# A selective state-space scan with routed experts on one core: the front re-ordered, the work at the half boundaries re-ordered, and the state update moved ahead of the partition sum in the steps that scatter rows

## What is computed

```python
dt   = soft_clamp(softplus(xn @ Wdt.T + bdt), 0.001, 0.1, 0.5)
B, C = xn @ WB.T, xn @ WC.T
A    = -exp(soft_clamp(A_log, -5, 5, 0.5))
dA   = exp(soft_clamp(dt[..., None] * A, -8, 8, 0.5))
for t in range(1024):                        # the scan; h is (batch, channel, state)
    h = dA[t] * h + dt[t] * B[t] * x[t]
    h = h * min(20 / (norm(h) + 1e-8), 1)    # norm over all channels and states of a batch
    y[t] = h @ C[t] + Dp * x[t]
# experts: top 2 of 8 by xn @ w_g, at most 1280 rows each, softmax of the two logits
out = combine(gelu(rows @ c_fc[e]) @ c_proj[e])      # for every expert e
```

## Time and profile before

| stretch | us | what |
|---|---|---|
| 0 to 69.67 | 69.67 | front |
| 69.67 to 93.06 | 23.39 | steps 0 to 15 |
| 93.06 to 305.70 | 212.64 | steps 16 to 143, with 64 scatters |
| 305.70 to 1454 | 1148.30 | steps 144 to 927 |
| 1454 to 1620 | 166.00 | the rest of the steps, 64 of them with a fetch |
| 1620 to 1644.40 | 24.40 | tail |

### The profile page before, as it was taken

One profiled execution on the slowest core, in us unless ns is written; L12 is line 12 of the kernel. 1 busy time (PEld: TensorE's weight loads), 2 busy tenths in 40 slices (PEclk: granted clock), 3 DMA queues, 4 the chain that ended last, 5 costly groups with the idle time before them and its releaser, 6 DMA issues.

```text
span 1644.4 us, 34338 instructions
## 1 busy us (share of the span) xinstructions
PE 1282.0 (78%) x9628; PEld 1123.2 (68%) x9628; DVE 1532.7 (93%) x9635; ACT 1153.7 (70%) x2909; POOL 777.6 (47%) x1253
## 2 busy tenths in 40 slices
PE   5656445479989888989989998898989798855661
PEld 4445344368878777877978787797878688844550
DVE  7688888999999999999999999999999999987788
ACT  5877456486787768868776877778777777847450
POOL 5166776544444443444443344344444444468852
PEclk9776677789999999999989999999999999967895
DMA  9921111200111020111002002011100200012245
GB/s 319 315 83 50 42 44 43 98 15 30 43 49 43 16 75 22 36 62 37 30 16 87 23 25 73 24 37 41 57 22 24 66 30 17 17 39 73 73 149 194
DMA packets 85088, 104.56 MB, mean 64 GB/s; under 512 B 7712, under 2 KB 75936, under 8 KB 84896
## 3 DMA queue, kind: packets, MB, share of 16 engines
q1 hardware_dynamic: 76848, 85.47, 15.8%
q0 software_dynamic: 6144, 16.79, 3.2%
q10 hardware_dynamic: 1904, 0.09, 0.1%
HBM read 56.45 MB, written 45.88 MB: 62 GB/s over the span
## 4 chain that ended last, share of the span: by engine, by line
PE 48%; POOL 15%; ACT 14%; DVE 14%; issue 7%; DMA 2%; ACTq 0%; POOLq 0%; SPq 0%; DVEq 0%
PE ps L1219 15%; PE ps L1203 13%; PE ps L1191 8%; POOL arena L516 7%; PE ps L1185 5%; ACT arena L854 4%; POOL xg L496 4%; PE ps L1153 3%; DVE arena L724 2%; DVE arena L702 2%; DVE arena L718 2%; DVE arena L710 2%; DVE arena L696 2%; POOL wf L502 2%; PE ps L1069 2%
## 5 line engine op out<-in xcount | busy, mean ns | idle before, releaser
L516 POOL TENSOR_TENSOR arena<-arena,neghalf 128x1 f32<-128x1 f32 x1025 | 602.3, 588 | 798.4 <-DVE arena L699 751.1
L724 DVE SCALAR_TENSOR_TENSOR arena<-arena 128x128 f32<-128x128 f32 x1024 | 360.5, 352 | 23.5 <-POOL arena L516 23.5
L1191 PE MATMUL ps<-arena,pick 128*128 128x128 f32 x2048 | 301.9, 295 | 49.4 <-ACT arena L961 25.7
L1203 PE MATMUL ps<-arena,wf 128*128 128x256 f32 x1280 | 308.9, 393 | 20.3 <-ACT arena L974 9.4
L1191 PEld LDWEIGHTS ps<-arena,pick 128*128 128x128 f32 x2048 | 279.0, 210 | 62.8 <-ACT arena L961 50.1
L961 ACT ACTIVATE arena<-ps,arena 128x128 f32<-128x128 f32 x1024 | 292.3, 374 | 32.6 <-PE ps L1191 30.7
L710 DVE CUSTOM_DVE_ANT_0 arena<-arena 128x128 f32<-128x128 f32 x1024 | 293.3, 286 | 9.5 <-PE ps L1153 5.8
L702 DVE CUSTOM_DVE_ANT_0 arena<-arena 128x128 f32<-128x128 f32 x1024 | 299.1, 292 | 2.2
L1219 PE MATMUL ps<-wp,arena 128*128 128x256 f32 x1280 | 295.8, 385 | 3.1 <-ACT arena L974 3.1
L696 DVE TENSOR_TENSOR arena<-arena 128x128 f32<-128x128 f32 x1024 | 290.6, 284 | 0.0
L1203 PEld LDWEIGHTS ps<-arena,wf 128*128 128x128 f32 x1280 | 244.7, 198 | 53.5 <-ACT arena L974 10.2
(11 more groups left out here) (148 smaller groups left out, 1323.3 us busy)
## 6 DMA issues: line engine op xcount, KB each, us to landing
xg<-zeros SPq DMA_DIRECT2D x10, 1024.0 KB, 10.6
xrow<-xg SPq DMA_DIRECT2D x40, 256.0 KB, 2.7
yg<-arena SPq DMA_DIRECT2D x40, 256.0 KB, 2.1
arena<-in_x SPq DMA_DIRECT2D x16, 512.0 KB, 8.8
wf<-in_c_fc SPq DMA_DIRECT2D x8, 1024.0 KB, 5.1
wp<-in_c_proj SPq DMA_DIRECT2D x8, 1024.0 KB, 6.0
ys<-arena SPq DMA_DIRECT2D x66, 64.0 KB
xnd<-arena SPq DMA_DIRECT2D x8, 512.0 KB, 5.7
```

What stands on the lines that cost most here:

```text
L516: g.tensor_tensor(sv[:, slot, 1:2], mx, neghalf[:, 0:1], ALU.pow).then_inc(s_ready, 1)
L724: v.scalar_tensor_tensor(hr[:, slot, :], vv, sv[:, before, 1:2], ur[:, slot, :], ALU.mult, ALU.add)\
L1191: last = t.matmul(ps[2][:, j * P:(j + 1) * P], pick[:, q * QUAD + j, :], xin, start=True, stop=True)
L1203: last = t.matmul(ps[4 + j % 2][:, c * TS:(c + 1) * TS], wf[:, k, (2 * j + c) * P:(2 * j + c + 1) * P], xt[:, k, :], start=k == 0, stop=k ...
```

## The change

It has four groups of edits.

1. **Front.** The small loads are issued in another order (A_log and the two vectors first). GpSimd needs 12 constants instead of 17 before it turns to the powers; the select that builds `pick` is cut into four of 512 columns, placed behind the powers of chunks 2 to 5, and the others behind that of chunk 1. The state ring and the windows are no longer cleared by GpSimd but by ScalarE (`clear_states`, 128 by 2048 twice, and one copy for `win`). VectorE normalises chunk 0 before the statistics of chunk 1. TensorE makes the time rates of half 0 ahead of the second transposes. ScalarE's list is re-ordered, and of half 0 it takes only the Tanh of steps 0 to 15 ahead of the scan (`tanh_part`, 128 by 64); those of steps 16 to 63 (128 by 192) follow in quads 0 to 2. In the routing the softmax of the two logits moves behind the slots.
2. **First blocks.** The Tanh of half 1 go into quads 3 to 14 instead of 0 to 14; rates and logs of half 2 go from quads 1 and 2 to quads 5 and 6.
3. **Half boundaries.** `logs_of` is split: `rates_out`, which frees the PSUM bank, now comes ahead of two `decay_op`. The soft clamp moves from the end of a half's third block to its second quad. Input pieces start 3 steps later and avoid steps with a scatter or fetch while others are free.
4. **Steps with a scatter.** The update comes ahead of the partition sum; `following` of such a step moves into the next one, behind its product, and the next step's maximum behind its first reduction.

```diff
-                    if step in sending:
-                        dve.wait_ge(q_ready, now)
-                        v.tensor_scalar(mx, qv, 1.0, None, ALU.max).then_inc(m_ready, 1)
-                    dve.wait_ge(h_ready, now)
-                    v.tensor_tensor(vv, hr[:, before, :], da[:, slot, :], ALU.mult).then_inc(v_ready, 1)
-                    if step not in sending:
-                        dve.wait_ge(q_ready, now)
-                        v.tensor_scalar(mx, qv, 1.0, None, ALU.max).then_inc(m_ready, 1)
+                        maximum(now)
+                    product(slot, before, now)
+                    if step - 1 in sending:
+                        following(slot - 1, (slot - 2) % RING, now - 1)
+                    if step not in sending and step - 1 not in sending:
+                        maximum(now)
                     v.tensor_tensor_reduce(out=junk[:, 0, :], in0=vv, in1=ur[:, slot, :], ...
+                    if step - 1 in sending:
+                        maximum(now)
                     ...
                     v.tensor_tensor_reduce(out=junk[:, 1, :], in0=vv, in1=vv, ...
+                    if step in sending:
+                        update(slot, before, now)
                     ...
                     v.tensor_reduce(out=terms[:, slot, 0:2], ...
+                    if step in sending:
+                        continue
+                    if step - 1 in sending or step + 1 in sending:
+                        dve.wait_ge(s_ready, now)
                         following(slot, before, now)
+                        update(slot, before, now)
+                    else:
+                        update(slot, before, now)
                         following(slot, before, now)
```

```diff
@@ statistics and normalisation
             statistics(0)
-            for i in range(CH):
+            normalize(0)
+            statistics(1)
+            dve.wait_ge(a_exp, 1)
+            v.tensor_scalar(a16[:, :], alog, -DT_K / 16.0, None, ALU.mult).then_inc(a_ready, 1)
+            for i in range(1, CH):
@@ GpSimd
-            g.memset(hr, 0.0).then_inc(h_ready, 1)
-            g.memset(win, 0.0).then_inc(init_win, 1)
@@ ScalarE, front
             turned(0)
-            turned(1)
-            logits_out(0)
-            logs_of(0, PREP_BANKS[0])
...
+            skip_of(0)
+            skip_of(1)
+            rates_out(0, PREP_BANKS[0])
+            logs_of(0)
+            turned(1)
+            clear_states(BLK).then_inc(h_ready, 1)
+            rates_out(1, PREP_BANKS[1])
+            logs_of(1)
...
-            tanh_ops(0, 12, 20).then_inc(tanh_done, 1)
+            tanh_part(16, 16, 0, BLK).then_inc(tanh_done, 1)
@@ ScalarE, in the blocks
+                    if blk % 4 == 0 and 0 < blk and q == 0 and blk // 4 + 2 < HALVES:
+                        rates_out(blk // 4 + 2, 6)
                     if blk % 4 == 0 and 0 < blk and q == 0:
                         for c in range(2, 4):
                             decay_op(f, c)
                     if blk % 4 == 0 and 0 < blk and q == 0 and blk // 4 + 2 < HALVES:
-                        logs_of(blk // 4 + 2, 6)
+                        logs_of(blk // 4 + 2)
+                    if quad < 3:
+                        last = tanh_part(11 * quad, min(11, 32 - 11 * quad), BLK, HALF)
...
+                    if blk % 4 == 2 and q == 1 and blk // 4 + 2 < HALVES:
+                        soft_clamp(blk // 4 + 2)
+                    if blk == 1 and q == 1:
+                        rates_out(2, 6)
+                        logs_of(2)
-                if blk % 4 == 2 and blk // 4 + 2 < HALVES:
-                    soft_clamp(blk // 4 + 2)
@@ TensorE, front
             turn(0)
+            time_rates(0, PREP_BANKS[0])
+            turn(1)
+            time_rates(1, PREP_BANKS[1])
```

## The result

| | before | after |
|---|---|---|
| median of the runs | 1648.2 us (4 runs beside after) | **1628.56 us** (1622.73 to 1632.95, 4 runs) |
| profiled execution, its span | 1646.17, 1644.4 | 1631.96, 1630.2 |
| steps 0 to 16 / 16 to 144 | 23.51 / 212.62 | 24.19 / 211.55 |
| steps 144 to 928 | 1148.2 | 1146.8 |
| steps 928 to 1023, rest | 165.3, 24.2 | 165.4, 24.2 |

The ratio is 0.9874 [0.9856, 0.9893]: 20 us faster, 1.3%. The table's stages are distances between partition sums, one of which stands in each step; the same stage sums are used for the experiments.

The account below looks back on a forecast made before the run. Bound by the scan's chain through the vector engine, held up by the front, 64 scatters through GpSimd and 13.3 us of stalls; -16.3 + 2.7 - 3.7 - 5.0 = -22.3, so 1624 us, range 1614 to 1637 for 8 in 10.

Parts of the forecast that it names:

- Front: Before step 0: it starts at 53.4 instead of 69.67, 16.3 us saved, between 11 and 18.
- First blocks: Start of the scan: moved Tanh and the wait for block 0's store give back 2.7 us, range 0 to 8.
- Half boundaries: Stalls of the scan at half boundaries: early rates and earlier clamp save 5.0 us, range 2 to 6.4.
- the arrival of the logits: In the front: the logits arrive at about 37.4 instead of 46.98, 9.6 us earlier.
- The store's wait: First blocks: the scalar engine waits 8 to 10 us near 84 for block 0's output store, with a stall in step 19.
- the first scatter's rows: First blocks: rows land at 76 and are wanted at 79, so the wait costs nothing, at the worst 2 us.
- Scatter steps: Pairs of steps with a scatter: a shorter scale saves 0.07 a pair, 53 pairs, 3.7 us.
- rival (c): Scatter steps: the update holds up the scatter, a pair grows by 0.38, total 1652 us; chance 0.04.
- The term of the rates: Half boundaries: rates emptied before two decay Exp shrink the 2.30 stall to some 0.5 and remove one of 0.76.
- that of the clamp: Half boundaries: the clamp in an earlier quad and pieces three steps later remove 3.8 us of stalls.
- the stall at step 832: Half boundaries: the 2.30 us stall behind TensorE shrinks to some 0.5, kept by the scalar engine's own lateness.

Follow-up runs that it names:

- the alteration that took them back: Changed kernel with each chunk's logits emptied ahead of turning the chunk two further on, in the front alone; 1626.52 us, ratio 0.9872 to the kernel before.
- Rates alone: Changed kernel with soft clamp and input pieces as in the kernel before, time rates still emptied ahead of two decay Exp; 1625.98 us.

## Why the prediction was right, and where not

The forecast of 1624 was 4.6 us below the median, which lies inside the range, with the right sign. Of the 4.6, 2.0 are the starting point: I counted from a profiled execution of 1646.17, and the median beside the change was 1648.2. The rest is 22.3 us of gain forecast and 19.6 seen. By its own steps:

**Front: 16.3 forecast, 12.45 seen; the step that failed is the arrival of the logits.** The first normalisation (8.0 forecast, 8.11), logits to ranks (8.3, 8.35), ranks to step 0 (7.65, 7.64), the short Tanh (0.22, 0.24) and the 192-column ones (0.34, 0.36) came as worked out. The logits came at 41.23 instead of 37.4. Of these 3.8 us, 1.4 had arisen by the first emptied rates (16.64, not 15.2): eight matmuls cost 3.78. I had halved the 5.41 of sixteen, of which the first ones already ran at the half rate: with 1.89 for the second eight, 3.5 are left for the first. Another 1.0 to 1.2 were the ring of waits between `logits_out` and the transposes, shown by the alteration that took them back. I had only summed ScalarE's list and even taken 0.7 of waits off. The last 1.2 to 1.4 stay open; with the better order ScalarE still waits 0.65 to 0.68 for TensorE in three chunks.

**First blocks: 2.7 forecast, 1.8 seen by step 32, by another mechanism.** Steps 0 to 16 grew by 0.69 and steps 16 to 32 by 1.12. The store's wait was there, 6.48 for a forecast of 8 to 10, but cost 0.47 ahead of one reduction. The rest is in scatters that wait for earlier ones (1.61 before one), and stayed when the store's wait was taken away. The size was near by luck. I had priced the first scatter's rows, and not the landing of its neighbours beside SyncE's next load. The term also moves with the front's: 1.4 us more of front left 0.2 at step 32. Had the logits come when I said, the first blocks would have given most of that back as well (an estimate from that one alteration), and the two terms together would have missed all the same: 13.6 forecast, 10.6 seen at step 32.

**Scatter steps: 3.7 forecast, 0.4 to 2.3 seen; a term was left out.** The second scale fell from 0.72 to 0.56, but the scatter rose from 1.04 to 1.15, and 0.03 a pair remained of 0.07. It is the milder form of my rival (c), whose sign I had and whose chance I had set low by the fetches: there an update starts 0.14 ahead of an indirect DMA that takes 1.08. I had set that row against the rival and then put its 0.04 at nothing; here it was 0.11, of the 0.16 that the scale gave. The scatter is 1.04 when the update starts behind its start and 1.12 to 1.15 when it starts 0.11 to 0.15 ahead. The rule of the Trainium skill (SBUF — State Buffer, SBUF: two separate sides), that a vector instruction with two SBUF inputs and a GpSimd instruction that reads SBUF exclude each other and the one that starts first wins, has the direction of what is seen here. It does not have the size: held up until the update's end the scatter would be 0.24 longer, and it is 0.11. Nor do the traces bear out the other half: in the kernel before the update starts 0.18 behind the scatter's start, in the midst of its 1.04, and takes 0.31, held up by nothing.

**Half boundaries: 5.0 forecast, 8.6 to 9.2 seen by medians, for half of the reason.** The term of the rates was too small and that of the clamp too large. I had given the early rates 2.6 and the clamp with its pieces 3.8. Rates alone make 11.1 (1637.12 to 1625.98), and the clamp's move with the pieces' no gain: by medians the run is 2.6 slower with it, which the intervals don't tell from zero. I had read the waits at input pieces as the clamp's own cost. They were in part ScalarE running late out of the boundary: with the rates alone early, 1.4 of the 3.8 went in one profiled execution and all of it in another. Whether the clamp in an earlier quad delays that quad's contributions is open; with it these waits came to anything from 2.1 to 8.1 us. I had also forecast 0.5 in place of the stall at step 832; the profiled execution has 1.18 and 1.56 there, where TensorE fell to its lower clock, and that of the kernel with the scatter steps as before has none. Of the 5.0 the profiled execution itself shows only 1.4 (1148.2 to 1146.8); it is the medians that show the term.

Against the forecast the front was 3.9 us worse, the first blocks 0.9 better, the scatters 1.4 to 3.3 worse and the halves 3.6 to 4.2 better. A part of the errors cancelled, so the total is nearer than its terms.

## What to carry to other kernels

When two engines hand work back and forth, sum neither engine's list alone: lay both queues side by side and look for an instruction that waits in front of one that the other engine needs. When several stalls have different releasers, ask which of them are one lateness carried on; mend the earliest and measure again before moving the rest. Follow what a gain at the start leaves at a later point, past the transfers that run beside it: 1.4 us at step 0 were 0.2 at step 32. And where an engine's slack at a boundary is as small as what a lower TensorE clock costs there (2.8 us), one profiled execution does not tell what an edit is worth; the medians of several do.

## What the runs showed of the hardware that I had not expected

- An indirect DMA issued by GpSimd takes 1.04 us when VectorE's two-input update starts behind its start, and 1.12 to 1.15 when it starts 0.11 to 0.15 ahead and still runs. The update that starts 0.18 behind such a DMA's start takes 0.31, no longer than in a plain step (0.35).
- GpSimd's power on 128x1 takes 0.56 to 0.58, or 0.71 to 0.72. The sum's place does not decide: 0.56 with the sum 0.37 behind, 0.72 with it 0.34 behind the earlier trace rows. In the three kernels with some 50 scales of 0.71 or more (the one before, and two with its scatter steps) one of the two reductions along the columns starts within some 0.01 us of nearly each of them, in the others 0.03 or more away; whether that is the cause was not tried.
- A scatter that is in flight beside a 512 KB load lands just behind it, 4.7 us after its issue instead of 2.6.
- VectorE's update starts 0.035 us after the end of the GpSimd scale that it waits for.
- After the same idle time of 3.10 us TensorE ran the same sixteen matmuls once at 1.2 and once at 2.4 GHz.
- At the start, behind 9.64 us of idle time, eight time-rate matmuls took 3.78 us and the next eight 1.89, at a granted clock of 1.00 in both stretches: the granted clock does not tell of every half rate.
